# Attention and routed experts on one core: projections of a unit on one PSUM bank, the other bank as a third bank for scores, and four banks in the last unit

## The reference, cut to what matters

```
x = L0_attn_x                                   # 8 batches, 1024 rows, 512 columns, float32
Q, K, V = (x @ W.T for W in (W_Q, W_K, W_V))    # 16 heads of 32
attn = where(causal, Q K^T / sqrt(32), -inf)
y = softmax(attn) @ V
x = layernorm(x + y @ W_O.T)
logits = x @ router_w.T + router_b              # 8 experts
out = (x @ expert_w[top1].T + expert_b[top1]) * max(softmax(logits))
return layernorm(x + out)
```

## Time and profile before

| | |
|---|---|
| median of 3 runs | 2839.43 us (2835.78 to 2843.49) |
| profiled execution | 2852.97 us, its span 2851.2 us |
| PE busy | 2597.9 us (91%) |
| DVE busy | 1404.0 us (49%) |
| ACT busy | 1038.3 us (36%) |
| POOL busy | 869.3 us (30%) |
| mean granted TensorE clock | 0.95 of 2.4 GHz |

### The profile page before, as it was taken

The page is one execution under the profiler, slowest core; times in us unless marked ns, Lnnn a source line. Parts: engine busy times, 40 slices in busy tenths (PEclk is TensorE's granted clock), DMA queues, the critical chain, the costliest instruction groups (busy, mean ns, idle before and its releaser), DMA issues. The chain is left out here.

```text
span 2851.2 us, 50322 instructions
## 1 busy us (share of the span) xinstructions
PE 2597.9 (91%) x15360; PEld 1606.0 (56%) x15361; DVE 1404.0 (49%) x2587; ACT 1038.3 (36%) x2089; POOL 869.3 (30%) x1532
## 2 busy tenths in 40 slices
PE   2999999999999999999999999999999999926998
PEld 2654575447554765466544755476546654425887
DVE  2555345634554366434653455336643565236665
ACT  2244423441345224432344134522443244413333
POOL 2222232223222232323222322323232321233665
PEclk9998999999999999999999999999999999958999
DMA  8422152314331242215231433124221421035443
GB/s 288 123 77 65 60 162 67 100 50 121 113 90 53 67 150 71 82 48 159 71 93 53 127 105 90 56 71 148 69 98 41 141 70 61 23 117 170 146 155 118
DMA packets 131017, 282.97 MB, mean 99 GB/s; under 512 B 33026, under 2 KB 42242, under 8 KB 128452
## 3 DMA queue, kind: packets, MB, share of 16 engines
q1 hardware_dynamic: 100920, 208.62, 24.1%
q0 software_dynamic: 28304, 70.64, 8.2%
q10 hardware_dynamic: 1536, 0.53, 0.1%
HBM read 133.04 MB, written 47.53 MB: 63 GB/s over the span
## 5 line engine op out<-in xcount | busy, mean ns | idle before, releaser
L673 ACT ACTIVATE probs<-score 128x512 f32<-128x512 f32 (+3 forms) x1536 | 708.8, 490 | 869.4 <-PE score L979 858.3
L727 DVE TENSOR_REDUCE tile_max<-maxp 128x1 f32<-128x512 f32 (+3 forms) x1072 | 678.4, 657 | 583.0 <-PE maxp L968 430.4
L979 PE MATMUL score<-q_stack,k_stack 97*128 97x512 f32 (+2 forms) x1536 | 589.3, 414 | 31.4 <-ACT probs L673 29.6
L964 PE MATMUL maxp<-k_stack,q_stack 96*128 96x512 f32 (+2 forms) x1360 | 522.4, 412 | 47.0 <-DVE tile_max L727 43.4
L920 PE MATMUL proj<-xt,w_qk 128*128 128x512 f32 x1536 | 462.8, 418 | 60.3 <-DMA w_qk<-w_qk_parts 49.9
L544 POOL TENSOR_SCALAR_AFFINE_SELECT probs<-probs 128x256 f32<-128x256 f32 x512 | 209.0, 409 | 871.7 <-ACT probs L673 871.5
L964 PEld LDWEIGHTS maxp<-k_stack,q_stack 96*128 96x128 f32 x1360 | 270.8, 199 | 275.7 <-DVE tile_max L727 141.4
L979 PEld LDWEIGHTS score<-q_stack,k_stack 97*128 97x128 f32 x1536 | 291.4, 198 | 232.8 <-ACT probs L673 184.2
L920 PEld LDWEIGHTS proj<-xt,w_qk 128*128 128x128 f32 x1536 | 296.4, 199 | 116.0 <-DMA w_qk<-w_qk_parts 49.6
L999 PE MATMUL y_ps<-probs,v 128*32 128x512 f32 (+3 forms) x3072 | 337.0, 512 | 1.8 <-DVE rows L751 1.4
L999 PE MATMUL den_ps<-probs,ones_f 128*32 128x512 f32 (+3 forms) x3072 | 330.2, 503 | 0.0
(11 more groups left out here) (136 smaller groups left out, 2137.7 us busy)
## 6 DMA issues: line engine op xcount, KB each, us to landing
w_qk<-w_qk_parts SPq DMA_DIRECT2D x64, 512.0 KB, 3.6
q_stack<-w_vo_parts SPq DMA_DIRECT2D x16, 2048.0 KB, 8.0
q_stack<-parts SPq DMA_DIRECT2D x512, 64.0 KB, 2.4
k_stack<-parts SPq DMA_DIRECT2D x512, 64.0 KB, 2.3
got<-dispatched SPq DMA_DIRECT2D x75, 257.0 KB, 2.7
xt_raw<-x_t SPq DMA_DIRECT2D x32, 512.0 KB, 4.1
q_stack<-parts POOLq DMA_DIRECT2D x256, 64.0 KB, 2.3
k_stack<-parts POOLq DMA_DIRECT2D x256, 64.0 KB, 2.3
```

The costliest lines, as they stand in the source:

```text
L673: nc.scalar.activation(probs[:, 4 * (n % PROBS) + h, c:BANK], score[h % 2][:, c:BANK], ACT.Exp, scale=SCALE).then_inc(exp_done.sem, 1)
L727: nc.vector.tensor_reduce(tile_max[:, j, heads[0]:heads[-1] + 1, qb], tiles, AX.X, ALU.max)\
L964: mm = nc.tensor.matmul(bank[:, place * cols:to], q_st[u % SETS][0:3 * DH, h, qb * P:(qb + 1) * P], k_st[u % SETS][0:3 * DH, h, j * BANK:j ...
L979: nc.tensor.matmul(score[h % 2][:, c0:BANK], k_st[u % SETS][0:3 * DH + 1, h, kb * P:(kb + 1) * P], q_st[u % SETS][0:3 * DH + 1, h, t * BAN ...
```

## The change

Scores get a third bank in units 0 to 2, `proj1`; all projections and transposed maxima of units 1 to 3 made inside the units use `proj0` alone. In unit 2, where nothing is projected, the maxima of unit 3 go round `maxp0`, `maxp1` and `proj0`. In unit 3 the scores go round `score0`, `score1`, `maxp0`, `maxp1`. So a score waits for the exponential three tiles before (four in unit 3), and a tile of maxima of unit 3 for the reduction three before. On ACT `high` stands behind the exponential of h = 1 of the group in which the projection ends; on DVE `low` follows in that same group, behind two maxima (and behind `divide`) instead of three. In unit 3 the product with ones stands directly behind that with the values, as in the other units.

```diff
+        jobs = alternating(OPENING + [("m", 0), ("v", 7)], 1)
         for u in range(1, UNITS):
-            job_names += [("p", u + 1, i) for i in range(4)] * (u + 1 < UNITS) + [("m", u)]
+            jobs += [(("p", u + 1, i), 0) for i in range(4)] * (u + 1 < UNITS) + [(("m", u), 0)]
+        jobs += alternating([("o", i) for i in O_GROUP.values()], 1)
...
-            return (maxp + score)[i % 4] if u == 0 else maxp[i % 2]
+            return max_ring(u)[i % len(max_ring(u))]
+
+        def max_ring(u):
+
+            return maxp + score if u == 0 else maxp + proj[0:1] if u == UNITS - 1 else maxp
+
+        def score_bank(u, i):
+
+            ring = score + maxp if u == UNITS - 1 else score + proj[1:2]
+            return ring[i % len(ring)]
+
+        def score_passed(u, i):
+
+            return max(STILES * u + i - 2, 0) if u < UNITS - 1 else STILES * u + max(i - 3, min(i - 2, -1))
...
-                        if u + 2 < UNITS:
-                            for i in tiles_made(j):
-                                high(b, u + 2, i)
+                            if u + 2 < UNITS and h == 1:
+                                for i in tiles_made(j):
+                                    high(b, u + 2, i)
...
-                        for i in due[0:3]:
+                        for i in due[0:2]:
                             reduce_tile(u + 1, i)
                         if u and j == LAG + 1:
                             divide(2 * u - 1)
-                        if u + 2 < UNITS and j:
-                            for i in tiles_made(j - 1):
+                        if u + 2 < UNITS:
+                            for i in tiles_made(j):
                                 low(b, u + 2, i)
-                        for i in due[3:]:
+                        for i in due[2:]:
...
-                    pe.wait_ge(free.sem, free.at(b, n // 2 if u else max(n // 2 - 1, 0)))
+                    pe.wait_ge(max_free.sem, max_free.at(b, MTILES * u + max(i + 1 - len(max_ring(u)), 0)))
...
-                    pe.wait_ge(exp_done.sem, exp_done.at(b, max(i - 1, 0)))
-                    nc.tensor.matmul(score[h % 2][:, c0:BANK], k_st[u % SETS][0:3 * DH + 1, h, kb * P:(kb + 1) * P],
+                    pe.wait_ge(exp_done.sem, exp_done.at(b, score_passed(u, i)))
+                    if u == 0 and i == len(score):
+                        wait_job(pe, b, proj_free, ("v", ROWT - 1))
+                    nc.tensor.matmul(score_bank(u, i)[:, c0:BANK], k_st[u % SETS][0:3 * DH + 1, h, kb * P:(kb + 1) * P],
...
                             if n >= LAG and h == 1:
                                 weigh(n - LAG, False)
-                            if n >= LAG and h == (3 if u == UNITS - 1 else 1):
                                 weigh(n - LAG, True)
```

More of the change, by code:

```diff
@@ L239, in attend @@
         xt_low = signal("xt_low", KT)
-        proj_full = [signal(f"proj_full{i}", JOBS // 2, AHEAD // 2) for i in range(2)]
-        proj_free = [signal(f"proj_free{i}", JOBS // 2, AHEAD // 2) for i in range(2)]
         part_high = signal("part_high", NPROJ, 4)
@@ L247, in attend @@
         max_full = signal("max_full", UNITS * MTILES)
-        max_free = [signal(f"max_free{i}", UNITS * MTILES // 2) for i in range(2)]
+        max_free = signal("max_free", UNITS * MTILES)
         max_step = signal("max_step", UNITS)
@@ L298, in attend, with alternating, on_bank @@
                       ("v", 4), ("v", 5)]
-        job_names = OPENING + [("m", 0), ("v", 7)]
+        LAST_CLOSING = [name for name in CLOSING if name[0] in "ox"]
+        def alternating(names, first):
+            return [(name, (first + n) % 2) for n, name in enumerate(names)]
+        jobs = alternating(OPENING + [("m", 0), ("v", 7)], 1)
         for u in range(1, UNITS):
-            job_names += [("p", u + 1, i) for i in range(4)] * (u + 1 < UNITS) + [("m", u)]
-        job_names += [("o", i) for i in O_GROUP.values()] + CLOSING
-        LAST_CLOSING = [name for name in CLOSING if name[0] in "ox"]
-        last_names = job_names[:-len(CLOSING)] + LAST_CLOSING
-        assert len(job_names) == JOBS and JOBS % 2 == 0 and AHEAD % 2 == 0 and len(AHEAD_JOBS) == AHEAD
+            jobs += [(("p", u + 1, i), 0) for i in range(4)] * (u + 1 < UNITS) + [(("m", u), 0)]
+        jobs += alternating([("o", i) for i in O_GROUP.values()], 1)
+        last_jobs = jobs + alternating(LAST_CLOSING, 0)
+        jobs += alternating(CLOSING, 0)
+        ahead_jobs = alternating(AHEAD_JOBS, 1)
+        assert len(jobs) == JOBS and len(ahead_jobs) == AHEAD
+        def on_bank(of, bank):
+            return [name for name, at in of if at == bank]
+        proj_full, proj_free = [[signal(f"proj_{state}{i}", len(on_bank(jobs, i)), len(on_bank(ahead_jobs, i)))
+                                 for i in range(2)] for state in ("full", "free")]
         def place_of(b, name):
-            names = AHEAD_JOBS if b is None else last_names if isinstance(b, int) else job_names
-            n = names.index(name)
-            return n % 2, n // 2
+            of = ahead_jobs if b is None else last_jobs if isinstance(b, int) else jobs
+            bank = dict(of)[name]
+            return bank, on_bank(of, bank).index(name)
         def wait_job(eng, b, sems, name):
@@ L954, in max_tile @@
                     qb, heads, j, cols, diag = MAX_TILES[i]
-                    n = MTILES * u + i
                     bank = max_bank(u, i)
-                    free = max_free[n % 2]
-                    pe.wait_ge(free.sem, free.at(b, n // 2 if u else max(n // 2 - 1, 0)))
-                    if n == 2:
+                    pe.wait_ge(max_free.sem, max_free.at(b, MTILES * u + max(i + 1 - len(max_ring(u)), 0)))
+                    if u == 0 and i == 0:
                         pe.wait_ge(exp_done.sem, exp_done.at(b, 0))
+                    if u == UNITS - 1 and i == len(maxp):
+                        wait_job(pe, b, proj_free, ("p", u, 3))
                     for place, h in enumerate(heads):
@@ L1016, in output @@
                     bank, full = begin(b, ("o", tb))
+                    if tb == 0:
+                        pe.wait_ge(exp_done.sem, exp_done.at(b, STILES * (UNITS - 1)))
                     pe.wait_ge(y_low.sem, y_low.at(b, tb + 1))
```

13 lines of the change are left out of this document (5 added, 8 removed).

## The result

| | before | after |
|---|---|---|
| median | 2840.15 us of 4 runs (2835.78 to 2843.49) | 2730.15 us of 4 runs (2722.56 to 2732.77) |
| profiled execution | 2852.97 us, span 2851.2 us | 2732.77 us, span 2731.0 us |

The ratio is 0.9609 [0.9586, 0.9632], 110 us less. That lies in the range, 15 us above the forecast of 2715, and has the forecast's sign. Span against span it is 120.2 us, or 15.0 a batch where the sum said 15.5.

A forecast was written before the change was run, and what follows sets the result against it. PE, busy 91% of the span, was taken as the bound. Terms summed to 15.5 us a batch, 124 in eight: 2852.97 to 2729, less 13.5 for the profiled execution's distance from the median, forecast 2715; range 2685 to 2775.

The forecast's parts named there:

- unit 3, four banks (with the copy of `y_ps`): Unit 3: four score banks remove 1.5 us of waits for exponentials a batch; 0.3 lost to the `y_ps` copy.
- unit 3, joined products: Unit 3: joining both products saves 0.34 us a full group, in twelve groups 4.1 us.
- third score bank, units 0, 1, 2: Ends of units 0 to 2: fewer score waits, saving 1.2, 1.3 and 1.4 us a batch.
- third maxima bank, unit 2: Unit 2: the long wait behind `divide` goes nearly whole, 1.0 us of other waits stays; 2.2 us saved.
- unit 2, clock: Unit 2: the 13.7 us fall to 1.2 GHz goes with the long wait, saving 5.5 us a batch.
- rival 3: Closing and opening: the other clock falls shrink too, 3.8 us a batch; 2685 us, chance 9%.
- Rival 2: ACT's latency sets scores: unit 3 gains 3 instead of 5.3, ends of units half; 2754 us, chance 12%.
- if the wait goes, I expect the clock to stay: Unit 2: without its wait of 1.62 us the clock stays full, worth 5.5 us a batch; called least certain.
- rival 1: Unit 2: the clock falls all the same, 10.0 us a batch gained; 2759 us, chance 17%.
- Rival 4: Slower: `low` waits for `high`, losing 7.2 us, and clocks fall in units 0 and 1; 2894 us, chance 4%.
- the prediction's own signs: In unit 2, no PE wait for DVE over 1 us; clock below 1.00 in units 0 or 1 refutes.
- The single projection bank costs nothing more: Projections: the bank is needed again 5 us later, and `low` ends 2 us earlier than that; cost nothing.

The follow-up runs named there:

- e8_banks_only: Changed kernel with unit 3's product with ones moved back behind h = 3, four score banks kept: 2752.03 us, ratio 0.9704.
- e6_last_two_banks: Changed kernel with unit 3's scores on two banks again, products still joined: 2834.04 us, ratio 0.9879.
- e1_join_only: Kernel before with only unit 3's products joined, banks as before: 2899.35 us, ratio 1.0103.
- e7_two_score_banks: Changed kernel with scores of units 0 to 2 on two banks again, unit 3 keeping four: 2816.03 us, ratio 0.9804.
- e2_two_max_banks: Changed kernel with unit 3's maxima going round two banks again in unit 2: 2775.8 us, ratio 0.9678.
- r_after: Changed kernel again, unedited, on another chip than the first measurement: 2769.93 us, ratio 0.9647.
- e5_three_max_alone: Kernel before with only the third maxima bank in unit 2 added: 2845.69 us, ratio 0.9925.
- e4_split_moved: Changed kernel with ACT's split of `x` in unit 2 behind h = 1 of groups 2, 3, 6, 7: 2740.0 us, ratio 0.9546.
- e9_low_first: The kernel of `e4_split_moved` with `low` behind one reduction of its group instead of two: 2727.64 us, ratio 0.9617.
- r_before: Kernel before once more, unedited, on a third chip: 2842.01 us in one run.

## Why the prediction was right, and which steps were not

The terms, us a batch (minus is time saved). Measured is the third batch after against before, or the run named:

| term | forecast | measured |
|---|---|---|
| unit 3, four banks (with the copy of `y_ps`) | -1.2 | -1.1 (`e8_banks_only`) |
| unit 3, joined products | -4.1 | -4.0 with four banks; with two +1.1 at full clock (`e6_last_two_banks`), +2.7 with a fall of the clock (`e1_join_only`) |
| third score bank, units 0, 1, 2 | -1.2, -1.3, -1.4 | -0.8, -1.4, -2.6 (`e7_two_score_banks`; unit 2 in the last batch) |
| third maxima bank, unit 2 | -2.2 | -2.7 (`e2_two_max_banks`, last batch); -1.8 in the others at equal clock |
| unit 2, clock | -5.5 | -5.5 in three of seven batches and the last; about 1.6 of it given back by a fall of 3.4 us in three of the others, 3.1 by one of 6.8 us in the fourth |
| ACT's split of `x` in unit 2 | not in the sum | +2.2 (44.65 against 42.46) |
| unit 1, whole | -0.1 | -0.4 |
| unit 0, whole | -1.0 | -0.7, and +0.8 in the three batches in which its clock fell |
| closing and opening | 0 | +0.1 (94.65 against 95.57 less the product's 1.00); in the first, sixth and seventh batch -2.7, -2.6 and -1.1 |

*The sum* was met in part by luck. Five of the eight batches are 13.2 to 13.9 us shorter, not 15.5. The mean of 15.0 comes from the first, the sixth and the last (18.2, 16.7 and 17.9). In the first two the closing and opening stretch runs at a clock of 0.98 and 1.00 instead of 0.95, which is rival 3 in a small form, and `r_after` shows nothing of it (97.1 to 101.6 us there); in the last, unit 3 of the kernel before had a fall of the clock. Unit 2 as a whole came to 9.3 us in the third batch where I had 9.1, because its waits were worth 2.4 more and the split of `x`, which I did not have, took 2.2. Rival 2's own sum was off too: its terms give 11.25 us a batch and not 10.6, so 2749 and not 2754.

*Unit 3* was right to 0.2 us, and its group to 0.01. The prices read from starts held in three kernels. Wrong was to count joining and banks as independent terms. Rival 2, ACT's latency behind bursts of four, is not what happens with four banks, but it is what `e1_join_only` and `e6_last_two_banks` show with two.

*Unit 2's waits* were mis-sized: 53.98 less 5.5 for the clock is 48.5 us, and without any disturbance the unit takes 42.5, so 6.0 us of waits went where I had 3.6. The runs show 2.6 of it for the score bank and 2.7 for the maxima bank. Of the 2.6, 1.95 lie at the unit's end, where I had 1.4 (from the last score tile of group 8 to the end 8.73 us in the last batch of the changed kernel, 10.68 in `e7_two_score_banks`), and 0.6 ahead of it, between the maxima, where I had nothing. The last 0.7 can't be put down to one part.

*Unit 2's clock*: the fall of 13.7 us has gone, as forecast. The maxima bank alone takes it away (`e5_three_max_alone`), and so does the rest of the edit without that bank (`e2_two_max_banks`). The step "if the wait goes, I expect the clock to stay" was half right. I asked what ends the wait, and not what comes next when the unit runs at full pace. The next was a load for the next batch, with nothing to spare. So rival 1 came true in a small form, by another wait. The Trainium skill's warning ("TensorE: Matmul & The Clock Gate", "A second HAM failure mode: psum-queue depth-cycling"), that cycling through banks lets the clock swing by small idle times, is borne out in one place and not in another. `e4_split_moved` cycles through three banks for maxima and three for scores at clock 1.00 through all of unit 2. But unit 3 of `e1_join_only` sends four score tiles in a row round two banks, and there the clock falls in all eight batches behind nothing but small waits. PE in the third batch, and the stretch behind:

```profile
910.59 0.93 PE L979 MATMUL score<-q_stack,k_stack 97*128 97x384 f32 x2 [0.45 <-ACT probs L673]
...
913.05 0.92 PE L979 MATMUL score<-q_stack,k_stack 97*128 97x256 f32 x2 [0.40 <-ACT probs L673]
...
913.60:916.90 3.30, 3.30 (x17) 0.66 (x17) 1.57 (x3) 0.64 (x2) 1.30 (x2) 0.50 0.74 293
```

`e6_last_two_banks` has such falls in three of eight batches, and the kernel before has one in unit 3 of its last batch (43.61 us at 0.96), behind waits of at most 0.34 us. So the prediction's reading, that the fall needs one long wait and that stretches with small ones are at 1.00, holds for its third batch and not in general. What is shown is that unit 2's falls begin during their one long wait or within 2 us behind it, and are gone from all eight batches of `e4_split_moved`, which has no such wait (its longest in unit 2 is 0.35 us).

*`low`*: the new waits for DVE in units 0 and 1 are there, 0.47 and 0.78 us in unit 1 (groups 1 and 5) where I had 0.9 each; over the eight batches unit 1 waits 15.3 us for maxima instead of 7.1, 1.0 a batch. So the place of `low` costs what I took in unit 1, within the 0.3 us by which the unit's total differs. In the profile after, PE's longest waits there, and in unit 0 the same in group 5, then the projection:

```profile
767.20 0.50 PE L987 MATMUL maxp<-k_stack,q_stack 96*128 96x512 f32 x1 [0.47 <-DVE tile_max L751]
...
788.92 0.50 PE L987 MATMUL maxp<-k_stack,q_stack 96*128 96x512 f32 x1 [0.78 <-DVE tile_max L751]
...
726.36 0.50 PE L987 MATMUL maxp<-k_stack,q_stack 96*128 96x512 f32 x1 [1.03 <-DVE tile_max L751]
...
704.27 1.19 PE L943 MATMUL proj<-xt,w_qk 128*128 128x512 f32 x4 [0.48 <-DVE parts L739]
...
727.70:731.10 3.40, 3.40 (x13) 1.93 (x16) 2.37 (x4) 1.05 (x3) 0.55 (x2) 0.50 0.64 173
```

Rival 4's mechanism, a clock fall in unit 0 behind a wait caused by `low`, is real, in three batches of eight (two in `r_after`) and at 1.5 us each instead of 5.5; it begins 1.3 us behind that wait each time. By the prediction's own signs, which allowed no clock below 1.00 in units 0 or 1 and no wait of PE for DVE over 1 us, the step that left these units at full clock failed. `e9_low_first` makes that wait longer (1.25 us), and there unit 0 of the third batch is at 0.97 too. The kernel before is not free of falls in unit 0 either: `r_before` has one in its fifth batch, elsewhere in the unit (46.7 us into it), behind waits of at most 0.47 us. "The single projection bank costs nothing more" was wrong by 0.5 us a batch (3.7 in eight places), in unit 0's first projection.

*The offset.* Against its own basis, the profiled execution, the sum gave 2729 and 2732.77 was measured. I then took off 13.5 us because the profiled execution before lay that far above its median. The one after lies 2.6 us above its own, so nearly the whole miss of 15 us is this subtraction. One profile's distance from the median is no property that a changed kernel inherits.

## What to carry to other kernels

Count a reordering and the buffers that it needs as one term, and ask what each does alone: joined products were worth 4.0 us with four banks and cost 1.1 to 2.7 with two. When a long wait or a slow clock is taken out of a stretch, look at every wait of every engine in it that is now within a microsecond of ending last, prefetches for the next iteration above all. Put such a prefetch's consumer where its load has surely landed, and if there is a choice not ahead of the work that PE waits for.

## What the runs showed of the hardware

One idle time of PE of 1.03 us (unit 0) or 2.1 to 2.5 us (unit 2) was followed by a granted clock of 0.50 for 3.4 us in some batches (6.8 in one batch of the changed kernel) and by none in others, with the same instructions around it; what decides between them is not settled. A fall of 3.4 us cost 1.5 to 1.6 us. Falls of 3.4 us also came behind waits of 0.45 us at most, once in a group of four score tiles, in every batch of `e1_join_only`. In the kernel before, one and the same wait of 1.62 us went with falls of 3.4, 10.2, 13.7 or 17.1 us in different batches (`before`, `r_before`), so the length of a fall is not set by the wait alone. And the same program differed by 1% between chips (2840 to 2871 us), nearly all of it, where two chips were compared, in the closing and opening, while undisturbed units repeated within 0.1 us (unit 0 within 0.3).
